# Dense softmax products of a graph network: two float32r parts made on the chip in place of three bf16 parts from a table

## The reference

```python
def _genconv(x, src, dst, W1, b1, g, be, W2, b2):
    msg = relu(x[src]) + 1e-07
    # softmax over the edges of each destination, value by value
    out = _softmax_aggregate(msg, dst, n) + x
    h = out @ W1 + b1                 # 128 -> 256
    h = relu(batch_norm(h) * g + be)
    return h @ W2 + b2                # 256 -> 128
for i in range(3):
    x = relu(_genconv(x, ...))
```

## Time and profile before

| | us |
|---|---|
| median of 3 runs | 4451.83 (4436.73 to 4454.9) |
| the profiled execution: time | 4460.21 |
| the profiled execution: span | 4458.4 |
| layer 0, first to last gather ended | 749.24 to 1416.72 |
| layer 1, first to last gather ended | 1478.8 to 2148.53 |
| layer 2, first to last gather ended | 2209.0 to 2879.39 |

### The profile page before, as it was taken

The page is one execution under the profiler, slowest core; times in us unless marked ns, Lnnn a source line. Parts: engine busy times, 40 slices in busy tenths (PEclk is TensorE's granted clock), DMA queues, the critical chain, the costliest instruction groups (busy, mean ns, idle before and its releaser), DMA issues. The chain is left out here.

```text
span 4458.4 us, 73923 instructions
## 1 busy us (share of the span) xinstructions
PE 3626.2 (81%) x22631; PEld 2451.3 (55%) x22631; DVE 1998.9 (45%) x5297; ACT 1185.7 (27%) x2569; POOL 2568.9 (58%) x2700
## 2 busy tenths in 40 slices
PE   2588887889897888999687989876788788878887
PEld 0355554545555544555554555575666666666665
DVE  6354433122223712131641222374566666666666
ACT  1232111000001500000420000173444444444444
POOL 4566554556664665666475666536556565555552
PEclk6798988999998989999898999897898989899888
DMA  6365445666664766666376666464444444444442
GB/s 244 119 203 166 135 137 171 199 192 210 206 216 126 242 196 192 215 208 203 123 252 191 203 206 215 152 189 132 115 126 126 123 129 123 125 125 126 123 128 66
DMA packets 347311, 744.31 MB, mean 167 GB/s; under 512 B 73666, under 2 KB 177276, under 8 KB 346339
## 3 DMA queue, kind: packets, MB, share of 16 engines
q0 software_dynamic: 134912, 331.04, 25.7%
q1 hardware_dynamic: 204295, 358.83, 25.1%
q10 hardware_dynamic: 7899, 51.90, 3.0%
HBM read 608.06 MB, written 133.44 MB: 166 GB/s over the span
## 5 line engine op out<-in xcount | busy, mean ns | idle before, releaser
L603 POOL DMA_INDIRECT ring<-split_table,src_idx x1240 | 1179.4, 951 | 735.0 <-issue 334.9
L1488 PE MATMUL ps<-spare,acc 128*128 128x500 fp8e4 x5292 | 1229.3, 385 | 201.1 <-issue 97.9
L2117 POOL DMA_INDIRECT ring<-h_table,idx_ring x832 | 822.3, 988 | 581.2 <-issue 276.1
L1488 PEld LDWEIGHTS ps<-spare,acc 128*128 128x128 bf16 x5292 | 521.0, 100 | 850.0 <-issue 280.2
L1589 DVE TENSOR_TENSOR onehot<-onehot,ps 128x168 f32<-128x168 f32 x165 | 54.3, 329 | 1268.9 <-PE ps L1499 775.0
L616 POOL DMA_INDIRECT adjacency<-acc x408 | 403.0, 988 | 308.3 <-issue 112.8
L1433 ACT ACTIVATE work<-ps 84x256 f32<-84x256 f32 x155 | 58.9, 380 | 1744.1 <-remote 1305.2
L1520 PE MATMUL ps<-ring,onehot 128*84 128x256 bf16 x3720 | 469.1, 281 | 47.1 <-issue 46.3
L1520 PEld LDWEIGHTS ps<-ring,onehot 128*84 128x84 bf16 x3720 | 416.0, 122 | 73.5 <-issue 69.5
L2127 PE MATMUL ps<-ident,ring 128*128 128x128 f32 x1664 | 296.7, 302 | 99.0 <-issue 74.1
L2166 PEld LDWEIGHTS ps<-mats,work 128*128 128x128 f32 x1664 | 244.8, 208 | 167.7 <-issue 166.1
(11 more groups left out here) (328 smaller groups left out, 4920.3 us busy)
## 6 DMA issues: line engine op xcount, KB each, us to landing
acc<-split_table SPq DMA_DIRECT2D x104, 768.0 KB
spare<-adjacency SPq DMA_DIRECT2D x108, 512.0 KB
e_few<-spare SPq DMA_DIRECT2D x104, 512.0 KB
acc<-e_few SPq DMA_DIRECT2D x208, 256.0 KB
work<-in_edge_attr SPq DMA_DIRECT2D x104, 256.0 KB
split_table<-acc ACTq DMA_DIRECT2D x32, 768.0 KB
ring<-split_table,src_idx POOLq DMA_INDIRECT x1240
adjacency<-Z ACTq DMA_DIRECT2D x6, 3136.0 KB
```

The lines of the kernel that those rows point to most:

```text
L603: e.indirect_dma_start(out=to, out_offset=None, in_=table, in_offset=bass.IndirectOffsetOnAxis(ap=src_idx[:, 2 * i + h, j:j + 1], axis=0)) ...
L1488: ins = e.matmul(ps[2 + 2 * c + kind][:, 0:width], split[j % 2][:, k, q, kind * D:(kind + 1) * D], moving, start=(b == q == 0), stop=(b == ...
L2117: e.indirect_dma_start(out=rows[:, s, j, :], out_offset=None, in_=h_table, in_offset=bass.IndirectOffsetOnAxis(ap=idx_ring[:, s, j:j + 1], ...
```

## The change

The dense products take two parts in float32r in place of three in bf16, and the parts are no longer read from `split_table`. SP loads the f32 rows of `msg_table` (256 KB a unit) and the counts. For a duo of two blocks ACT takes exp (`dense_exp`, 128x256), DVE multiplies (`dense_times`, 128x256), ACT copies the 128x512 values to float32r (`dense_high`), DVE subtracts that to give the low part (128x512). For every block ACT casts 128x1000 counts from fp8 to float32r (`cast_block`) into one of five buffers. PE does 2 chunks x 2 kinds x 2 parts = 8 matmuls a block, 1176 in a layer for 1764; its blocks wait for `d_low` and `cast`, and raise `dense` once a block. The blocks of step i+1 are prepared at the end of ACT's and DVE's step i. The blocks now run at 2.99 a step in steps 4 to 52. Copies of a finished region move into the duo after next (d % 25 == 1). In layers 1 and 2 the new loads wait until the three-part table is made and stored. The gathered side keeps its three bf16 parts, its 55 pairs and the border; it still needs `split_table`. The diff also carries renamed sizes, general code for a narrower last region (all regions stay 1000 wide), and moved scratch buffers.

```diff
-STEP_BLOCKS = 2.75
+CHUNKS = sum(len(widths) for _, widths in REGIONS)
+DUOS = -(-BLOCKS // 2)
+CASTS = 5
+FIRST_STEP = 4
+STEP_COLUMNS = 2990
...
-    return max(0, int((n - 3) / STEP_BLOCKS))
+    r, b = divmod(n, BLOCKS)
+    before = sum(BLOCKS * sum(widths) for _, widths in REGIONS[0:r]) + b * sum(REGIONS[r][1])
+    return FIRST_STEP + before // STEP_COLUMNS
...
+            under_acc.enter_context(nc.sbuf_tensor("under_acc", [P, 2 * NCH * D], F32))
+            two_parts = under_acc.enter_context(nc.sbuf_tensor("two_parts", [P, 2, 2, 2, 2 * D], F32R))
+            casts = under_acc.enter_context(nc.sbuf_tensor("casts", [P, CASTS - 1, 1000], F32R))
...
+            last_cast = under_ring.enter_context(nc.sbuf_tensor("last_cast", [P, 1, 1000], F32R))
...
+            def duos_at(i):
+                return [d for d in range(ALL_DUOS) if step_of(first_block(d)) == i + 1]
+
+            def space_made(e, S):
+                if not ready:
+                    e.wait_ge(S("v_low"), UNITS)
+                    for b in range(5):
+                        e.wait_ge(S(f"split_out{b}"), stored_units(max(u for u in range(UNITS) if made_in(u) == b)))
...
-                    reached(e, S("dense"), j - 1)
+                    width = sum(REGIONS[r][1])
+                    if j >= 2:
+                        e.wait_ge(S("cast"), last_block(j - 2))
...
+                def load_dense_rows(j):
+                    u = j % UNITS
                     n = blocks_of(u)
-                    reached(e, S("dense"), j - 1)
-                    if not ready and j < 4:
-                        e.wait_ge(S(f"split_out{j - 2}"), 16)
-                    if not ready and r == 0:
-                        e.wait_ge(S(f"split_out{made_in(u)}"), stored_units(u))
-                    e.dma_start(split[j % 2][:, 0:n, :, :].rearrange("p n q x -> p n (q x)"), split_by_block[:, u * UNIT:u * UNIT + n, :]
-                                ).then_inc(S(f"split_in{j % 2}"), 16)
-
+                    if j >= 2:
+                        e.wait_ge(S("d_mul"), duos_through(j - 2))
+                    e.dma_start(dense_rows[j % 2][:, 0:n, :], by_block[:, u * UNIT:u * UNIT + n, :]).then_inc(S(f"dense_rows_in{j % 2}"), 16)
...
+                    for u in range(4, UNITS):
+                        load_rows(u)
+                    e.wait_ge(S("v_low"), UNITS)
+                    load_dense_rows(0)
+                    load_dense_rows(1)
+                for j in range(2, ALL_UNITS):
+                    load_dense_rows(j)
...
+                def dense_exp(d):
+                    n = first_block(d)
+                    j, k = unit_of(n), n % BLOCKS % UNIT
+                    m = end_block(d) - n
+                    if d == 0:
+                        space_made(e, S)
+                    if k == 0:
+                        e.wait_ge(S(f"dense_rows_in{j % 2}"), 16 * (j // 2 + 1))
+                    reached(e, S("d_low"), d - 1)
+                    e.activation(dense_values[d % 2][:, 0:m, 0:D], dense_rows[j % 2][:, k:k + m, :], ACT.Exp, bias=negc[:, :]
+                                 ).then_inc(S("d_exp"), 1)
+
+                def dense_high(d):
+                    m = end_block(d) - first_block(d)
+                    e.wait_ge(S("d_mul"), d + 1)
+                    if d >= 2:
+                        e.wait_ge(S("dense"), end_block(d - 2))
+                    e.activation(two_parts[:, d % 2, 0:m, 0, :], dense_values[d % 2][:, 0:m, :], ACT.Copy).then_inc(S("d_high"), 1)
+
+                def cast_block(n):
+                    r = n // BLOCKS
+                    j, k = unit_of(n), n % BLOCKS % UNIT
+                    width = sum(REGIONS[r][1])
+                    if k == 0:
+                        e.wait_ge(S(f"counts_in{j % 2}"), 16 * (j // 2 + 1))
+                    reached(e, S("dense"), n - CASTS + 1)
+                    e.activation(cast_counts[n % CASTS][:, 0:width], counts[j % 2][:, k, 0:width].bitcast(F8), ACT.Copy).then_inc(S("cast"), 1)
+
+                def keep_products(r):
+                    for c, width in enumerate(REGIONS[r][1]):
+                        e.wait_ge(S("dense"), BLOCKS * (r + 1))
+                        reached(e, S("evacuated"), 2 * (r - 1) + c + 1)
+                        e.activation(products[c][:, 0:width], ps[3 + 2 * c][:, 0:width], ACT.Copy).then_inc(S("product_kept"), 1)
+
+                def dense_duo(d):
+                    if d == 0:
+                        dense_exp(0)
+                    if d + 1 < ALL_DUOS:
+                        dense_exp(d + 1)
+                    if d > DUOS and d % DUOS == 1:
+                        keep_products(d // DUOS - 1)
+                    cast_block(first_block(d))
+                    dense_high(d)
+                    for n in range(first_block(d) + 1, end_block(d)):
+                        cast_block(n)
...
+                    for d in duos_at(i):
+                        dense_duo(d)
...
-                    u, k = divmod(b, UNIT)
-                    j = UNITS * r + u
-                    if k == 0:
-                        e.wait_ge(S(f"counts_in{j % 2}"), 16 * (j // 2 + 1))
-                        if ready:
-                            e.wait_ge(S(f"split_in{j % 2}"), 16 * (j // 2 + 1))
-                        elif j < 2:
-                            e.wait_ge(S("v_low"), u + 1)
-                        else:
-                            e.wait_ge(S(f"split_in{j % 2}"), 16 * (j // 2))
+                    d = r * DUOS + b // 2
+                    e.wait_ge(S("d_low"), d + 1)
+                    e.wait_ge(S("cast"), n + 1)
...
-                        moving = counts[j % 2][:, k, at:at + width].bitcast(F8)
                         for kind in range(2):
-                            for q in range(3):
-                                ins = e.matmul(ps[2 + 2 * c + kind][:, 0:width], split[j % 2][:, k, q, kind * D:(kind + 1) * D], moving,
-                                               start=(b == q == 0), stop=(b == BLOCKS - 1 and q == 2))
+                            for q in range(2):
+                                ins = e.matmul(ps[2 + 2 * c + kind][:, 0:width], two_parts[:, d % 2, b % 2, q, kind * D:(kind + 1) * D],
+                                               cast_counts[n % CASTS][:, at:at + width], start=(b == q == 0), stop=(b == BLOCKS - 1 and q == 1))
                         at += width
-                    if k == blocks_of(u) - 1:
-                        ins.then_inc(S("dense"), 1)
+                    ins.then_inc(S("dense"), 1)
...
+                def dense_times(d):
+                    n = first_block(d)
+                    j, k = unit_of(n), n % BLOCKS % UNIT
+                    m = end_block(d) - n
+                    e.wait_ge(S("d_exp"), d + 1)
+                    e.scalar_tensor_tensor(out=dense_values[d % 2][:, 0:m, D:2 * D], in0=dense_rows[j % 2][:, k:k + m, :], scalar=EPS_MSG,
+                                           in1=dense_values[d % 2][:, 0:m, 0:D], op0=ALU.add, op1=ALU.mult).then_inc(S("d_mul"), 1)
+
+                def dense_duo(d):
+                    m = end_block(d) - first_block(d)
+                    if d == 0:
+                        dense_times(0)
+                    if d + 1 < ALL_DUOS:
+                        dense_times(d + 1)
+                    if d > DUOS and d % DUOS == 1:
+                        keep_divisors(d // DUOS - 1)
+                    e.wait_ge(S("d_high"), d + 1)
+                    e.tensor_tensor(two_parts[:, d % 2, 0:m, 1, :], dense_values[d % 2][:, 0:m, :], two_parts[:, d % 2, 0:m, 0, :].bitcast(F32),
+                                    ALU.subtract).then_inc(S("d_low"), 1)
```

More of the change, by code:

```diff
@@ L109, in dense_jobs @@
     return out
-JOBS = [j for j in dense_jobs() if j[0] < PAIRS]
-LATE = [j for j in dense_jobs() if j[0] >= PAIRS]
+JOBS = [j for j in dense_jobs() if j[0] < PAIRS - 1]
+LATE = [j for j in dense_jobs() if j[0] >= PAIRS - 1]
 TAIL = [[(node, least, sparse) for _, node, least, sparse in LATE if sparse and least < PAIRS],
-        [(node, least, sparse) for _, node, least, sparse in LATE if not sparse and least == 2 * len(REGIONS) - 1],
-        [(node, least, sparse) for _, node, least, sparse in LATE if not sparse and least == 2 * len(REGIONS)],
+        [(node, least, sparse) for _, node, least, sparse in LATE if not sparse and least == CHUNKS - 1],
+        [(node, least, sparse) for _, node, least, sparse in LATE if not sparse and least == CHUNKS],
         [(node, least, sparse) for _, node, least, sparse in LATE if sparse and least == PAIRS]]
@@ L249, in gnn_kernel @@
         HITS = (COLS + NEAR + 1) // 2
-        same = [second[:, at + k * HITS:at + (k + 1) * HITS].bitcast(BF16) for k in range(4)]
-        at += 4 * HITS
+        same = [onehot[:, k, :, :].rearrange("p j w -> p (j w)")[:, 0:HITS].bitcast(BF16) for k in range(4)]
```

(39 more changed lines are left out.)

71 lines of the change are left out of this document (34 added, 37 removed).

## The result

The changed kernel takes 4430.3 us in the median of 18 runs, the kernel before 4449.8 in 18 runs beside it: ratio 0.995, interval 0.9935 to 0.9965, about 20 us (16 to 29 from the interval's ends) less. Forecast were 52 less and a range of 4130 to 4490. The time came out where the rival "no change" had put it (4434), by other terms than that rival's.

A forecast was written before the change was run, and what follows sets the result against it. It took POOL's gather batch plus the lag in seeing PE's increments (11.87 us a pair) as the bound. 4460.2 - 47 - 15 + 10 = 4408, less 8.4 from profiled run to median, gave 4400; range 4130 to 4490.

The forecast's parts named there:

- the rival "no change": Whole kernel: dearer gathers take what waits give back, 4434, or PE gains no slack, 4462 us; chance 0.17.
- What bounds the kernel: Edge phases: POOL's batch plus the lag in seeing PE's increment, 10.02 + 1.85 = 11.87 us a pair; PE isn't in it.
- The first rival: POOL's gaps between batches fall to 0.30 us, 274 us more gain, 4126; chance 0.20 wholly or in part.
- I take all 47 us: POOL's long waits in three layers: PE, with 3.5 us to spare a step, catches up and all 47 us go.
- By my reading the 11.87 stays: POOL's ordinary steps: batches stay 11.87 us apart, with no gain there from fewer matmuls.
- By 5 each: 15: PE's tails after the last gathers, 14.6, 13.9 and 9.2 us, shrink by 5 each as no backlog remains: 15 us.
- So I take 10: POOL's gathers beside busier DVE: dearer by 10 us in all, as DVE's share rises from 0.22 to about 0.37.
- the first bound: POOL's gathers beside busy DVE: 988 ns against 951, 44 us over 147 steps x 8.
- On-chip parts at nothing: ACT's and DVE's added casts, exps, copies and adds cost nothing, covered by 6 us of idle ACT per step.
- The slower rival: `dense` increments seen as late as `sums`, a batch lost at six switches, 71 us: 4518, or 4482 with half; chance 0.18.
- The sum: Whole kernel: 47 of long waits and 15 of tails less, 10 of gathers more: 4408 profiled, 4400 against the median 4451.8.

The follow-up runs named there:

- the half rows: Kernel before with only the dense blocks' new schedule, its gathers cut to half a row from pair 8 on: 4415.2 us beside 4453.9, ratio 0.9912 (late increments).
- schedule alone: Kernel before with only the changed schedule of dense blocks (none before step 4, then 2.99 a step), three bf16 parts kept: 4378.8 us, ratio 0.9901.
- two of three parts: Kernel before without the third bf16 part in the dense products, 8 matmuls a block, nothing made on the chip: 4371.0 us, ratio 0.9886.
- high parts alone: Changed kernel without the matmuls by the low parts, 4 a block in place of 8: 4345.2 us beside 4421.7 for the kernel before, ratio 0.9817.

## Why the prediction was wrong

**What bounds the kernel: right, for this kind of chip.** PE's increments are seen when POOL's batch has been issued, mostly 1.5 to 2.0 us after it, and the pace is batch plus lag. The changed kernel (11.8 apart with PE's step near 9), the one with still fewer matmuls, and the half rows all show it. The first rival, POOL's pace falling to its own, would have needed gaps of 0.3 throughout; they came so only on the other chips. What the trace couldn't tell is that this is not a fact of the kernel but of the chip it ran on.

**"I take all 47 us" of long waits: 22, and 39 came from elsewhere.** POOL's idle time fell by 64: 3 before the first gather of layer 0, 61 in the 162 gaps between batches. Gaps of over 3.4 us were nine with 77 us in all and are eleven with 59; beyond an ordinary gap of 2.07 they held 58 and now hold 36, so 22 less. The other 39 lie in the ordinary gaps, which the prediction left as they were ("By my reading the 11.87 stays"): their mean was 1.93 and is 1.67, the median 2.11 and 1.91, and 29 for 17 are so short (under 1 us) that the sums must have been seen before the batch ended. How much of the 39 is the change's doing is open. In the first group the median goes from 2.00 (schedule alone) over 1.92 (two of three parts) to 1.83 (high parts alone), so less work for PE shortens it a little; but the schedule-only kernel has 2.00 there and its half-row twin 2.13 in the last group.

**The cause of the long waits was the failed step.** The prediction put them down to PE's falling behind under its load. The schedule alone shortens them as much, by 23 to 29 us, and I had costed it at nothing but the missing blocks at step 0. And the three waits of 11.5 to 13.4 us at the first switch of each layer aren't backlog. The kernel before, around 991.91 in the earlier trace rows:

```profile
962.28 5.23 PE L1488 MATMUL ps<-spare,acc 128*128 128x500 fp8e4 x24
984.12 4.75 PE L1488 MATMUL ps<-spare,acc 128*128 128x500 fp8e4 x12 [16.61 <-DMA spare<-adjacency]
...
981.80 0.59 ACT L1415 ACTIVATE numerators<-ps 128x500 f32<-128x500 f32 x1 [13.84 <-remote]
```

PE ended the region at 967.51. ACT's copy, which waits for `dense`, starts at 981.80, 14.3 us later and 3.1 after POOL's batch had ended, and PE stands idle for it. In layers 1 and 2 it is 14.0 and 14.2 us. That is the lag again, on another semaphore. In the changed kernel it is still there, at the second switch of layer 1:

```profile
1914.75 0.61 PE L1567 MATMUL ps<-casts,two_parts 128*128 128x500 f32 x2
1929.36 3.44 PE L1567 MATMUL ps<-casts,two_parts 128*128 128x500 f32 x8 [14.01 <-DVE acc L1715]
...
1928.43 0.59 ACT L1479 ACTIVATE numerators<-ps 128x500 f32<-128x500 f32 x1 [8.34 <-remote]
...
1935.84 0.94 POOL L615 DMA_INDIRECT ring<-split_table,src_idx  x1 [10.24 <-PE ps L1598]
```

Other long waits of the changed kernel (4.4 us at 1058.10 and 1248.63, 5.2 at 2296.37) each end 0.3 us behind a group of sums that took 13 to 20 us, the slow stretches of the last section.

**"By 5 each: 15" of tails: failed.** From the last gather to the end of the last sums it was 14.6, 13.9 and 9.2 us; it is 13.4, 13.9 and 13.5. The timeline of PE there:

```profile
1390.83 2.79 PE L1598 MATMUL ps<-ring,onehot 128*84 128x256 bf16 x24
1402.39 0.54 PE L1577 MATMUL ps<-ident,work 84*128 84x84 f32 x2 [8.77 <-ACT work L1518]
...
1410.71 2.78 PE L1598 MATMUL ps<-ring,onehot 128*84 128x256 bf16 x24
```

PE isn't behind with work; it waits 8.8 us for ACT's copy of sums that it ended at 1393.6, because the last batch of gathers is still being issued. The tail is the lag, once more: on a chip of the second kind it is 3.6 us in layer 0, before and after the change alike. My own finding, applied there, would have said so.

**"So I take 10" for dearer gathers: 22.** The mean per gather rose by 18 ns, half-way between nothing and the first bound of 37. I scaled it by DVE's busy share and took a quarter of the bound. The Trainium skill (GPSIMD Engine Reference, section "1. Specifications") names DVE instructions with two SBUF inputs as ones that contend with GpSimd. The runs fit it, since cutting both such instructions down brings 970 back to 950 ns; no run puts another kind of DVE work in their place. The first bound, 44 us, was not reached.

**On-chip parts at nothing: right for ACT.** Casts take 1.03 us, ACT is busy 245 of 648 us, and no wait of PE for a cast is among its longest. PE's pace is 16 matmuls in 3.7 us, 0.23 each against 0.22 taken, so the weight load of 188 ns (the median) is hidden. The rule on fast weight load (the Trainium skill, TensorE: Matmul & The Clock Gate, section "Weight-path perf modes — Fast Weight Load (FWL) and DoubleRow") holds for the load, and costs nothing here.

**The slower rival: its mechanism is there, its price isn't.** PE waited for `d_low` 0.2 us in all. But `dense` is seen as late as `sums` at the switches: PE stood 50 us there in six waits, the longest the 14.0 above. Of the 71 us that the prediction priced, POOL's gaps show 8 in one switch and 3 in another (10.2 and 5.2 us for 2.07), and the kernel before had paid more at its own (13.2, 11.5 and 13.4).

**The sum.** The three gather phases are 38 us shorter (61 less between batches, some 23 more of gathers) and the tails 3 longer, so 35 by rows; the profiles differ by 44 (the other 9 lie outside the gather phases and tails), the medians by 20. For the phases the forecast said 37 less (47 and 10), which came out by luck: the long waits were taken 25 too high and the gathers' price 13 too low, against 39 us of ordinary gaps that stood at nothing. What made the sum of 52 too high by rows is the tail term, 15 less for 3 more. The last 15 between rows and medians no trace places. They are of the size that ordinary gaps change by between two groups of runs on one chip: 0.13 us in 150 gaps are 20 us, an estimate.

## What to carry to other kernels

When waits end on "remote" a fixed time behind another engine's bursts, and not behind the work that should release them, look for it in every wait on that engine, tails and switches too, and ask whether it belongs to the kernel or to the chip: run the unchanged kernel on a second chip before tuning to it. The schedule that gained on one kind lost on the other in the two kernels that carried it. Count a change on the queue that paces the stage in two columns, idle and busy; here one fell and the other rose on both kinds of chip. And when matmuls are traded for vector work, price what that work does to an engine beside it, instruction by instruction.

## What the runs showed of the hardware

Two kinds of chip under the same program: the kernel before takes 4422 and 4454 us in two groups of runs on one chip, and 4450 in the main comparison; it takes 3668 to 3673 on the three others. With the same one chip late at both ends of the series and three others prompt between them, the difference looks like one of the chip; what it is in the chip isn't shown. Nearly all of it is idle time of POOL before its indirect DMAs, in every phase: 735.0 us for 416.9 before the gathers of the softmax layers, 581.2 for 268.1 in the edge layers, 308.3 for 176.6 in the setup, 763 of the 788 between the two profiled executions.

On the first kind, ACT and POOL see PE's increment of the sums 4 to 8 us after its matmuls in an ordinary step and 13 in the earlier trace rows, mostly 1.5 to 2.0 us behind the last gather that POOL has issued (now and then 1.0, and a few times in the midst of a batch), whatever the gathers' bytes and whichever of the two waits. Where POOL is already idle it is prompt: in eight steps of the kernel before's layer 0 the sums end over 2.3 us behind a batch, and ACT's copy starts 0.04 us after them. ACT's own increments are seen within 0.3 us. DVE sees PE's transposes within 0.3 us in 14 of 35 cases of the kernel before between 1000 and 1400 us, all while a batch is being issued, so not every increment of PE is late; which are and why stays open.

On the first kind PE also has slow stretches with nothing that the profile names: in the changed kernel's layer 0 four groups of 24 sums take 10.6 to 13.4 us in place of 2.8, and in layer 2 one takes 20.1. On the second kind the changed kernel's sums take up to 8.1 us in the run shown above, and there the rows name waits for gathered data; the kernel before's take 3.2 at most.
